# Block loads of their own step, one cast and one maximum moved, and an addition handed from VectorE to GpSimd

## The reference

```
h = relu(layernorm(x));  W[src, dst] += edge_weight
x = x + h @ W.T + bias0
h = relu(layernorm(x))
for (Ws, Wn, b) in two layers:          # relu after the first
    mean = segment_sum(h[src], dst) / max(degree, 1)
    h = h @ Ws + mean @ Wn + b
out = x + h
```

## Time and profile before

| | |
|---|---|
| three runs | 824.78, 825.89, 826.84 us; median 825.89 |
| the profiled execution | 826.84 us, its span 825.1 us |
| busy share | TensorE 97%, VectorE 57%, ScalarE 46%, GpSimd 47% |
| granted TensorE clock, mean | 0.998 of full speed |

### The profile page before, as it was taken

The page is one execution under the profiler, slowest core; times in us unless marked ns, Lnnn a source line. Parts: engine busy times, 40 slices in busy tenths (PEclk is TensorE's granted clock), DMA queues, the critical chain, the costliest instruction groups (busy, mean ns, idle before and its releaser), DMA issues.

```text
span 825.1 us, 13564 instructions
## 1 busy us (share of the span) xinstructions
PE 798.2 (97%) x4660; PEld 647.1 (78%) x4661; DVE 469.8 (57%) x799; ACT 378.3 (46%) x491; POOL 384.3 (47%) x558
## 2 busy tenths in 40 slices
PE   3999999999999999999999999999999999999998
PEld 2666788888888878887887878888877888878786
DVE  7999666657542677856623453232556757336443
ACT  6755653443354222222336876543222333257653
POOL 3000056556735688756661210114788676724311
PEclk9999999999999999999999999999999999999999
DMA  3122335565464863556865653555753669758654
GB/s 108 43 69 82 99 116 177 172 182 170 159 234 159 275 207 105 181 202 216 319 219 180 196 175 102 179 175 178 268 170 116 196 212 332 253 180 281 209 170 138
DMA packets 82520, 148.57 MB, mean 180 GB/s; under 512 B 9973, under 2 KB 21356, under 8 KB 82448
## 3 DMA queue, kind: packets, MB, share of 16 engines
q1 hardware_dynamic: 62506, 102.68, 39.2%
q10 hardware_dynamic: 18422, 40.05, 13.7%
q0 software_dynamic: 1520, 4.92, 1.5%
HBM read 100.34 MB, written 47.27 MB: 179 GB/s over the span
## 4 chain that ended last, share of the span: by engine, by line
PE 73%; POOL 8%; issue 5%; DMA 4%; DVE 4%; ACT 4%; SPq 1%; ACTq 0%; POOLq 0%; DVEq 0%
PE bank L1306 28%; PE bank L1334 19%; PE bank L1243 13%; POOL T L848 3%; PE bank L1161 3%; PE bank L1150 3%; DMA stage<-hT_scratch 3%; PE bank L1166 2%; POOL T L846 2%; ACT split L1009 1%; PE bank L1145 1%; POOL S L817 1%; POOL S L813 1%; ACT Ax L1041 1%; PE bank L1350 1%
## 5 line engine op out<-in xcount | busy, mean ns | idle before, releaser
L1306 PE MATMUL bank<-slot,split 128*128 128x512 f32 x1680 | 388.6, 392 | 2.9 <-POOL split L831 1.2
L1306 PEld LDWEIGHTS bank<-slot,split 128*128 128x128 f32 x1680 | 314.5, 188 | 71.6 <-issue 3.0
L793 POOL TENSOR_TENSOR AT<-AT,az 128x50 int32 (+3 forms) x288 | 84.6, 294 | 141.3 <-DMA az<-asum_scratch 102.6
L831 POOL TENSOR_TENSOR split<-stage,split 128x512 fp32r<-128x512 f32 x50 | 64.5, 1292 | 141.3 <-ACT split L1009 141.3
L1612 DVE TENSOR_TENSOR slot<-T,slot 128x512 fp32r<-128x512 f32 x64 | 71.5, 1117 | 95.6 <-ACT slot L1000 91.1
L1041 ACT CAST Ax<-AT 128x1280 fp32r<-128x1280 uint16 x40 | 106.8, 2674 | 31.6 <-PE bank L1334 21.1
L1612 DVE TENSOR_TENSOR slot<-wst,slot 128x512 fp32r<-128x512 f32 x48 | 45.8, 980 | 84.8 <-ACT slot L1000 84.8
L1243 PE MATMUL bank<-slot,split_m 128*128 128x512 f32 x320 | 89.6, 394 | 0.0
L1000 ACT CAST slot<-T 128x512 fp32r<-128x512 f32 x64 | 40.0, 624 | 107.3 <-POOL T L848 80.6
L1334 PE MATMUL bank<-slot,Ax 128*128 128x512 f32 x320 | 77.2, 393 | 0.5 <-ACT Ax L1041 0.5
L1721 DVE SCALAR_TENSOR_TENSOR cst<-bank,dinv,stage 128x512 f32<-128x512 f32 x40 | 30.0, 751 | 73.9 <-PE bank L1334 73.4
(11 more groups left out here) (170 smaller groups left out, 1035.3 us busy)
## 6 DMA issues: line engine op xcount, KB each, us to landing
stage<-hT_scratch SPq DMA_DIRECT2D x90, 256.0 KB, 3.8
wst<-in_L_gnn_W_neigh SPq DMA_DIRECT2D x56, 256.0 KB, 4.0
wst<-in_L_gnn_W_self SPq DMA_DIRECT2D x56, 256.0 KB, 3.2
x1b_scratch<-x ACTq DMA_DIRECT2D x10, 512.0 KB, 5.0
hT_scratch<-hTs ACTq DMA_DIRECT2D x10, 512.0 KB, 3.2
stage<-prod0s_scratch SPq DMA_DIRECT2D x20, 256.0 KB, 2.9
hT_scratch<-h1s ACTq DMA_DIRECT2D x20, 256.0 KB, 3.5
stage<-prod1s_scratch SPq DMA_DIRECT2D x20, 256.0 KB, 2.8
```

Source lines behind the costliest of these rows:

```text
L793: pool.tensor_tensor(a, a, az32[:, n % NZ, pairs * pos:pairs * (pos + 1)], ALU.add) \
L831: pool.tensor_tensor(split[:, v % 2, 1, :], source(v), split[:, v % 2, 0, :].bitcast(F32), ALU.subtract).then_inc(s_olo, 1)
L1306: last = pe.matmul(dense_bank(v, which)[:, :], split[:, v % 2, a, NT * k:NT * (k + 1)], slot[t % 2][:, b, HF * (HK * which + k):HF * (HK * ...
```

## The change

SP's loop loads the blocks of step v in step v instead of those of v+1, so that operand v+2 comes ahead of the blocks of v+1. ScalarE casts operand 1 at the start of step 0 instead of in the mixing. The maximum of the degrees moves to steps 33 and 34, and the register load into `by_weight`, behind product 34 on TensorE and behind `sub_products(34)` on VectorE. In layer 1 POOL adds the bias b1 into the loaded base (`base_and_b1`), one tile ahead, and signals `s_bb`; VectorE adds that sum in one operation.

```diff
--- before.py
+++ after.py
-AT_TOP = 20
...
+        s_bb = sem("s_bb")
@@ -528,14 +528,10 @@
         def rows_of(i):
             return NL if i == TN - 1 else NT
 
-        def greatest_degree(eng):
+        def by_weight(eng, later):
 
             eng.wait_ge(s_top, 1)
             degree, = load(eng, top[0:1, :], 0, E)
-            return degree
-
-        def by_weight(eng, degree, later):
-
             with eng.If(degree > EXACT):
                 later(True)
             with eng.If(degree < EXACT + 1):
@@ -690,12 +686,9 @@
             for n in units_begun_in(1 + TN):
                 load_asum(n)
             for layer in range(2):
-                for c in blocks_at(VL * layer):
-                    load_block(c)
                 for v in range(VL * layer, VL * (layer + 1)):
-                    if v + 1 < VL * (layer + 1):
-                        for c in blocks_at(v + 1):
-                            load_block(c)
+                    for c in blocks_at(v):
+                        load_block(c)
                     if v + 2 < VL * (layer + 1):
                         load_operand(v + 2)
                     for n in units_begun_in(1 + TN + v + 1):
@@ -856,6 +849,14 @@
                 pool.tensor_tensor(g[:, 1, :], g_staged(k), g[:, 0, :].bitcast(F32), ALU.subtract) \
                     .then_inc(s_glo, 1)
 
+            def base_and_b1(o):
+                half, n = divmod(o, TN)
+                if o == 0:
+                    pool.wait_ge(s_b0, 32)
+                pool.wait_ge(s_bs[o % 2], used(o, 2))
+                pool.tensor_tensor(base[:, o % 2, :], base[:, o % 2, :], b0[:, HF * half:HF * (half + 1)], ALU.add) \
+                    .then_inc(s_bb, 1)
+
             operand_lo(0)
             for layer in range(2):
                 for v in range(VL * layer, VL * (layer + 1)):
@@ -870,8 +871,12 @@
                 for k in g_at(layer, VL - 1):
                     g_lo(k)
                 for o in range(OL):
+                    if layer == 1 and o == 0:
+                        base_and_b1(0)
                     if layer == 1 and o >= 1:
                         store_out(pool, OL + o - 1)
+                    if layer == 1 and o + 1 < OL:
+                        base_and_b1(o + 1)
                     for k in g_between(layer, o):
                         g_lo(k)
                     if layer == 0 and o == OL - 1:
@@ -1024,7 +1029,6 @@
                 elif what == "T1":
                     if i == TN - 2:
                         operand_hi(0)
-                        operand_hi(1)
                     hT_out(i)
                     if i < WB:
                         block_hi(i)
@@ -1091,7 +1095,7 @@
 
             for layer in range(2):
                 for v in range(VL * layer, VL * (layer + 1)):
-                    if v + 1 < VL * (layer + 1) and v not in (0, VL):
+                    if v + 1 < VL * (layer + 1) and v != VL:
                         operand_hi(v + 1)
                     for c in blocks_at(v):
                         block_hi(c)
@@ -1354,10 +1358,8 @@
             for v in range(VL):
                 if 0 <= v - FIRST_DEG - 1 < TN:
                     degrees(v - FIRST_DEG - 1)
-                if v == AT_TOP:
+                if v == VL - 1:
                     greatest_degrees()
-                if v == AT_TOP + 2:
-                    degree = greatest_degree(pe)
                 product(v)
                 if v == 1:
                     turn_hn(TN - 1)
@@ -1374,7 +1376,7 @@
                 for o in range(OL, 2 * OL):
                     neighbours(o, heavy)
 
-            by_weight(pe, degree, later)
+            by_weight(pe, later)
 
         @block.vector
         def _(dve):
@@ -1701,14 +1703,16 @@
                     dve.wait_ge(s_ag, o)
                     dve.tensor_tensor(Axlo[:, :, :], ATd[:, NT * n:NT * (n + 1), :].rearrange("p d s -> p s d"),
                                       Ax[:, o % 2, :, :].bitcast(F32), ALU.subtract).then_inc(s_axlo, 1)
-                if rest_o == 0:
-                    dve.wait_ge(s_b0, 16 * (layer + 1))
+                if layer == 0:
+                    if o == 0:
+                        dve.wait_ge(s_b0, 16)
+                    add = b0[:, HF * half:HF * (half + 1)]
+                else:
+                    dve.wait_ge(s_bb, rest_o + 1)
+                    add = base[:, o % 2, :]
                 dve.wait_ge(s_sl[o % 2], used(o, 2))
                 sums = stage[:, o % 2, 1, :]
-                link(dve.tensor_tensor(sums, sums, b0[:, HF * half:HF * (half + 1)], ALU.add))
-                if layer == 1:
-                    dve.wait_ge(s_bs[o % 2], used(rest_o, 2))
-                    link(dve.tensor_tensor(sums, sums, base[:, o % 2, :], ALU.add))
+                link(dve.tensor_tensor(sums, sums, add, ALU.add))
                 if layer == 0 and o >= 2:
                     dve.wait_ge(s_t2, o - 1)
                 if layer == 1 and rest_o >= 2:
@@ -1724,16 +1728,14 @@
             for v in range(VL):
                 if 0 <= v - FIRST_DEG < TN:
                     count_edges(v - FIRST_DEG)
-                if v == AT_TOP - 1:
+                if v == VL - 2:
                     dve.wait_ge(s_deg, TN)
                     link(dve.tensor_scalar(degm[:, :], bank[6][0:NT, 0:TN], 1.0, None, ALU.max))
                     dve.reciprocal(dinv[:, :], degm[:, :])
                     dve.tensor_reduce(degmax[:, :], degm[:, :], AX_X, ALU.max).then_inc(s_dmax, 1)
-                if v == AT_TOP + 1:
+                if v == VL - 1:
                     dve.wait_ge(s_drow, 1)
                     dve.tensor_reduce(top[:, :], bank[6][0:1, 0:NT], AX_X, ALU.max).then_inc(s_top, 1)
-                if v == AT_TOP + 2:
-                    degree = greatest_degree(dve)
                 for c in blocks_at(v):
                     block_lo(c)
                 sub_products(v)
@@ -1752,7 +1754,7 @@
                 for o in range(OL, 2 * OL):
                     finish_tile(o, heavy)
 
-            by_weight(dve, degree, later)
+            by_weight(dve, later)
 
 
 def mix_order():
```

## The result

The changed kernel takes 832.99 us (median of 4 runs, 832.08 to 834.0); the kernel before, with one more run beside it, 825.34 (4 runs, 824.15 to 826.84). The ratio is 1.0092, interval 1.0069 to 1.0114: slower by 0.9%, where 0.4% faster was forecast. The profiled execution has a span of 831.3 us against 825.1, and a granted clock of 0.995.

A forecast was written before the change was run, and what follows sets the result against it. It took TensorE, busy 97% of the span, as the bound. Terms 4.7 + 1.5 - 1.0 - 0.25 - 1.7 gave 3.25 us faster, forecast as 822.8 us, range 820.6 to 826.4.

The forecast's parts named there:

- They bring a wait: Last stage, layer 1: POOL's additions hold `g_lo` until the base lands, delaying the last `load_g` and tile 11; cost 1.7 us.
- The *loop* rival: Last stage: POOL and SP's loop becomes the bound, deciding from a landing of 5.3 us; 828.6 us, chance 0.08.
- another rival: New idling ahead of product 1 or around tiles 10 and 11 lowers the clock: 824.4, two falls 826.1; chance 0.2.
- SP's order: Products of both layers: earlier operands remove waits and the slow clock; gain 4.7 us in layer 0, 1.5 in layer 1.
- The cast: Start of layer 0: operand 1's cast behind tile 9 of the mixing makes product 1 late; cost 1.0 us.
- Load and branch: End of layer 0: register load and branch start later, delaying the first neighbour matmul; cost 0.25 us.
- The rival "gain smaller": Layer 0: POOL or block loads are as late as the operand; only about 2 of 4.7 comes, 825.5, chance 0.15.

The follow-up runs named there:

- the wait alone: Kernel before, with POOL waiting for b1 and for each base as in the change but adding nothing: 825.39 us, ratio 1.0012.
- the run with `g_lo` first: Changed kernel with POOL taking `g_lo` ahead of the addition for the next tile: 824.59 us, ratio 1.0002.
- the work: Kernel before, with twenty POOL additions of 128x512 on a buffer nobody reads, with no wait for a load: 828.94 us, ratio 1.0062.
- the landing: Changed kernel with four base buffers in place of two, each base loaded two tiles earlier: 825.90 us, ratio 1.0023.
- the start: Changed kernel with b1 loaded early, in the products of layer 1, and two base buffers: 825.27 us, ratio 1.0004.
- order and start both changed: Changed kernel with b1 loaded early and `g_lo` ahead of POOL's addition: 822.67 us, ratio 0.9982.

## Why the prediction was wrong

The step that failed is "They bring a wait: in each tile POOL now holds `g_lo` ... until the base has landed", priced at 1.7 us (ends 0.6 and 4.5). It measured 11.0 in the traces, 10.3 in the runs with the addition alone. The term was right as a price of the wait alone (1.4, measured), and wrong as a price of the additions, because it followed one base near the turn of the halves as if all before it ran on time. They didn't. One cycle of the loop in the changed kernel, on the queue, POOL and VectorE:

```profile
768.14 0.43 SPq L654 DMA_DIRECT2D base<-x1b_scratch  x1
...
774.07 0.50 SPq L654 DMA_DIRECT2D base<-x1b_scratch  x1
775.48 0.32 SPq L638 DMA_DIRECT2D cst<-prod1g_scratch  x1
```

```profile
769.78 1.29 POOL L857 TENSOR_TENSOR base<-base,b 128x512 f32<-128x512 f32 x1 [3.33 <-DMA base<-x1b_scratch]
771.03 1.30 POOL L849 TENSOR_TENSOR slot<-cst,slot 128x512 fp32r<-128x512 f32 x1
...
779.44 1.26 POOL L857 TENSOR_TENSOR base<-base,b 128x512 f32<-128x512 f32 x1 [3.54 <-DMA base<-x1b_scratch]
780.67 2.94 POOL L849 TENSOR_TENSOR g_last<-cst,g_last 128x512 fp32r<-128x512 f32 x2
```

```profile
771.10 1.78 DVE L1715 TENSOR_TENSOR stage<-stage,base 128x512 f32<-128x512 f32 x1 [3.35 <-POOL base L857]
772.92 0.75 DVE L1725 SCALAR_TENSOR_TENSOR cst<-bank,dinv,stage 128x512 f32<-128x512 f32 x1
```

The reader is to follow tile 8. Its base has landed at 769.78; POOL adds for 1.29; VectorE's addition starts at 771.10, and POOL's `g_lo`, which stood behind the first addition, starts at the same moment beside it, so that it takes 1.78 in place of 0.69; the tile is finished at 773.67; only then may SP load the sums and the base of tile 10 (774.07), which takes until 779.44. That is 9.66 for two tiles, the three turns before it took 10.0, 9.4 and 9.4, and TensorE needs 2 x 4.53 = 9.07. So the loop falls behind with every pair. Without the 1.1 that VectorE's addition loses beside `g_lo` the 9.66 would be 8.6 (an estimate), under TensorE's pace; that fits the run with `g_lo` first, whose additions mostly take 0.69. In tile 10, the first that needs the second half's last `g`, SP's last `load_g` goes out at 775.48, 1.43 after the start of that tile, where before it went 2.56 ahead of its start (772.70 against 775.26): 4.0 late, not 1.7. Behind it stand the waits of 4.15 and 0.46, and the low clock on the end of tile 10 and on tile 11 comes on top.

The *loop* rival, given 0.08, was this mechanism with three things left out. It said that the loop decides from a landing of 5.3 us. It counted the issue, POOL's two operations and the landing, and not VectorE's addition and finish, 1.78 + 0.75, which stand between a base and the next load. It took the additions as if POOL and VectorE did not disturb each other: 1.1 of the 1.78. And it took 4.0 for a landing, from the earlier trace rows. The late start (b1) finishes tiles 0 and 1 within 1.4 us of each other, and from then on a tile's finish hangs on its base and not on TensorE: the loads go out in pairs, some 3.5 us apart, and from tile 4 on the first of each pair lands after 5.1 to 5.7. It also passed over the clock there, which another rival had, with 0.2.

The experiments give each link its weight. In the length of the stage the wait alone costs 1.4 and the work 6.1 (with VectorE's two additions kept), together 10 to 11. That each delays the other is what the loop says; the 6.1 is no share of the 11.0, since VectorE's load differs. POOL's order gives back 8.3 of the 11.0 in its trace and about 8 in the runs, the landing 8.4 and about 6, the start most of it in the median, but less than half in its one trace. With order and start both changed nothing is left in the trace.

A second term was mis-sized, SP's order, which the large one hid. The points beside the addition, each by its step:
- *SP's order.* The mechanism was right: operand 9 goes out at 270.87 (269.62 with the order alone; predicted about 270), its cast waits for no load, and products 9, 10 and 25 wait for nothing. The size was not. The sum has 4.7 + 1.5 for it, and the order alone is worth 4.1 in the runs. The 4.83 in layer 0 compare one execution with another, and the one of before was late there: its operand 9, issued at 275.05, was cast at 282.06, while in the four others with the old order and the old cast it was issued at 275.2 to 275.4 and cast at 279.8 to 280.8. The late issue alone does not make the waits of 0.63 and 1.57; in that execution a landing of 7.0 us came to it, where the others have 4.6 to 5.4. Layer 1's products take 187.57 (537.42 to 724.99), and took 189.02: 1.45, predicted 1.5, and 1.1 with the order alone; the five with the old order took 188.2 to 189.3.
- *The cast*: 1.0 in the trace, 1.3 in the runs; predicted 1.0. The 239.4 of the prediction is 239.5 by its own terms (237.31 + 0.76 + 1.27 + 0.2), and its 0.2 is read at product 15, where the wait ended with VectorE's `q`; product 14 gives 0.15.
- *Load and branch*: between 0.1 and 0.8 in the seven traces that have it (from product 34 to the first neighbour matmul: 6.50 after, 6.64 alone, 6.08 without POOL's addition, 6.82 at the most, against 5.98 for a pitch of 5.49 and the wait of 0.49 before); predicted 0.25. The branch's own time sets it, and not the queue.
- *The rival "gain smaller"*: blocks as late as the operand were not seen, but its number, about 2 in place of 4.7, is nearer to what the runs leave for layer 0 (4.1 less 1.1 or so) than the forecast was. That is luck, by another cause.

So the rest of the change, forecast at 4.95 faster, gave 2.2, and the addition, forecast at 1.7 slower, took 10.3. The range ended at 826.4 because the loop rival was held to be rare, and its 828.6 would still have been too low.

## What to carry to other kernels

An operation moved to an idle engine is priced by the loop that it joins: write down what must happen between one load into a buffer and the next load into it, engine by engine, with every operation, and compare that with the pace of the bound; a median landing is no price when loads come in pairs. Before a wait of one execution goes into a sum, look whether other executions have it. Put work that waits for a load behind the work in the same queue that does not. Twenty additions that VectorE made in its idle time cost nothing; on POOL, one place ahead of `g_lo`, they cost 10 us.

## What the runs showed of the hardware

VectorE's addition of two SBUF operands of 128x512 (f32) nearly stands still while POOL runs a `tensor_tensor`: 0.68 alone, 1.78 beside one of POOL's, 3.36 beside two, and POOL's stays at 1.30. 3.36 is 0.68 and the 2.55 that POOL's two take, and a little more. In that row VectorE had even started first, 750.44 against 750.69, and still did the waiting. VectorE's combination of a bank with one SBUF operand is not slowed: 0.75 at 772.92 with POOL's addition beside it, as everywhere:

```profile
772.86 1.30 POOL L857 TENSOR_TENSOR base<-base,b 128x512 f32<-128x512 f32 x1
```

The Trainium skill (GPSIMD Engine Reference, Specifications) names contention of the two engines for VectorE instructions with two SBUF inputs. The traces agree, and in the cases shown VectorE pays all of it.

The granted clock was 0.50 behind the 4.15 us of idling in tile 10. Shorter waits went either way. Those of 1.50 and 0.79 in the changed kernel and of 2.24 with four buffers (granted clock 1.000 over that whole run) were followed by no visible fall. Behind two that stood close together it fell: 1.57 with 0.63 ahead in the kernel before, 2.10 and then 0.94 with b1 early (0.50 from 779.5), 1.93 and then 0.35 with POOL's spare additions (0.50 from 781.1), where in the last two the matmuls between the waits still ran at full clock. What of a wait decides it stays open.
